# Values of three narrow attentions projected token-major and read back from DRAM into their block-diagonal tile

## What is computed

```python
qkv = x @ qkv_w.T + qkv_b                                  # [64, 17, 576]
qkv = qkv.reshape(B, N, 3, NUM_HEADS, hd).transpose(2, 0, 3, 1, 4)
q, k, v = (qkv[0], qkv[1], qkv[2])                         # 12 heads, hd = 16
attn = jax.nn.softmax(jnp.einsum('bhnd,bhmd->bhnm', q, k) * scale, axis=-1)
out = jnp.einsum('bhnm,bhmd->bhnd', attn, v)
out = out.transpose(0, 2, 1, 3).reshape(B, N, C) @ proj_w.T + proj_b
```

## Time and profile before

| | |
|---|---|
| median of 3 runs | 937.37 us (935.59 to 946.7) |
| the profiled execution | 934.18 us |
| its span | 932.1 us |
| stage a0 in the span | about 39 to 147 us |
| stage a2 | about 554 to 637 us |
| stage a3 | about 727 to 839 us |
| PE busy, DVE busy, ACT busy | 92%, 48%, 42% |

### The profile page before, as it was taken

The page is one execution under the profiler, slowest core; times in us unless marked ns, Lnnn a source line. Parts: engine busy times, 40 slices in busy tenths (PEclk is TensorE's granted clock), DMA queues, the critical chain, the costliest instruction groups (busy, mean ns, idle before and its releaser), DMA issues. The chain is left out here.

```text
span 932.1 us, 16890 instructions
## 1 busy us (share of the span) xinstructions
PE 854.9 (92%) x6194; PEld 608.5 (65%) x6195; DVE 447.4 (48%) x903; ACT 387.8 (42%) x857; POOL 186.7 (20%) x207
## 2 busy tenths in 40 slices
PE   6899888999998799999989789999999999999997
PEld 5556656677775467777668466765687566666776
DVE  5566676777744412222268666551104566633111
ACT  2366653453542022333243864554151455532332
POOL 0610003444500134445200012220000000002232
PEclk9999999999988899999999999999999999997999
DMA  8000000000004967112150019000000211102111
GB/s 294 1 2 1 1 2 0 1 2 1 1 2 102 256 182 198 46 51 46 39 164 3 0 45 258 6 2 28 1 1 1 56 50 50 52 19 97 43 51 34
DMA packets 30638, 51.07 MB, mean 55 GB/s; under 512 B 3750, under 2 KB 23752, under 8 KB 30572
## 3 DMA queue, kind: packets, MB, share of 16 engines
q1 hardware_dynamic: 22140, 36.09, 14.0%
q0 software_dynamic: 4416, 9.84, 3.8%
q10 hardware_dynamic: 4016, 4.23, 1.4%
HBM read 43.30 MB, written 6.83 MB: 54 GB/s over the span
## 5 line engine op out<-in xcount | busy, mean ns | idle before, releaser
L79 PE MATMUL banks<-con 128*128 128x512 f32 (+1 forms) x206 | 95.1, 572 | 3.0 <-DVEq L2136 1.4
L1846 PE MATMUL banks<-moe_wu,moe_xf 96*128 x256 | 92.1, 505 | 1.6 <-ACT moe_xf L1954 0.8
L634 PE MATMUL banks<-x,a_wqkv 96*96 96x272 f32 x288 | 74.6, 397 | 0.9 <-PEq L457 0.5
L1846 PEld LDWEIGHTS banks<-moe_wu,moe_xf 96*128 96x128 f32 x256 | 47.5, 195 | 31.4 <-issue 4.8
L944 ACT ACTIVATE a_vt<-banks 102x384 f32<-102x384 f32 x96 | 41.9, 488 | 50.4 <-PE banks L710 50.1
L154 ACT ACTIVATE ln_sq<-x 96x544 f32<-96x544 f32 x32 | 21.1, 658 | 93.2 <-DVE x L146 93.2
L634 PEld LDWEIGHTS banks<-x,a_wqkv 96*96 96x96 f32 x288 | 45.4, 164 | 18.2 <-issue 3.2
L79 PEld LDWEIGHTS banks<-con 128*128 128x128 f32 x206 | 38.4, 202 | 25.9 <-issue 22.4
L2151 DVE TENSOR_TENSOR moe_hid<-banks,moe_gs 128x384 f32<-128x384 f32 x32 | 17.9, 558 | 77.6 <-PE banks L1846 77.6
L710 PE MATMUL banks<-con,a_vx 96*102 96x96 f32 x384 | 42.7, 253 | 7.4 <-ACT a_vt L944 6.1
L2008 POOL DMA_INDIRECT moe_xs<-moe_x_rows,moe_taken x32 | 31.2, 974 | 76.1 <-PE banks L1830 54.2
(11 more groups left out here) (409 smaller groups left out, 1772.2 us busy)
## 6 DMA issues: line engine op xcount, KB each, us to landing
moe_wu<-in_moe_up SPq DMA_DIRECT2D x16, 576.0 KB, 8.9
f_w<-in_f_e SPq DMA_DIRECT2D x10, 576.0 KB, 14.6
moe_wd<-in_moe_down SPq DMA_DIRECT2D x16, 288.0 KB, 9.9
patch_px<-in_patches SPq DMA_DIRECT2D x4, 768.0 KB, 9.4
f_wu<-in_f_up SPq DMA_DIRECT2D x4, 582.0 KB
f_wd<-in_f_down SPq DMA_DIRECT2D x4, 576.0 KB
f_x_rows<-f_xtok ACTq DMA_DIRECT2D x4, 384.0 KB, 3.4
a_wqkv<-in_a_wqkv SPq DMA_DIRECT2D x3, 432.0 KB, 8.3
```

What stands on the lines that cost most here:

```text
L79: self.nc.tensor.matmul(self.ps[bank][:, 0:width], self.ident, self.con[:, 0:width], start=True, stop=True)
L634: last = nc.tensor.matmul(ps[2 + m][0:HD, 0:CW], wqkv[:, a, j * D + m * HD:j * D + (m + 1) * HD], chunk(x, c)[:, a], start=a == 0, stop=a ...
L1846: last = nc.tensor.matmul(ps[2 + 2 * p + u][:, 0:BW], xf[0:KU[a], p, a], wu[0:KU[a], bass.ds(e, 1), a, u * BW:(u + 1) * BW].rearrange("p e ...
```

## The change

- `vx`, `spread_values`, `project_v`, `turn_values` and the copies of `take_values` are gone. In their place `values(n)` projects values token-major for 9 tiles of 128 tokens in five groups (2, 1, 2, 2, 2 tiles), x as the weights and `wqkv`'s 192 value columns as the moving tile, into one PSUM bank; ACT copies a group to `vtok` [128 tokens, 192] in one instruction.
- SP writes each tile to a DRAM tensor `v_rows` [1088, 192] (96 KB a tile, 48 KB the last) and then reads the values back into `vt`, which now holds two whole chunks, [102, 2, 16, 2, 96]. For each chunk and each of the 12 heads there are two DMAs: one of 16 tokens x 16 images and one of the 17th token x 16 images, in pieces of 64 bytes. A chunk's read-back is 24 DMAs with 3,264 pieces. The first chunk's are shared: 12 from SP, 12 from ACT.
- The parts of `vt` off the diagonal are zeroed once a stage, by two POOL memsets of 102 x 3072.
- Columns of keys, scores and weights are ordered token by head (k h) and not head by token, so that the rows of `vt` of one head are 6 partitions apart. Maxima and sums of DVE read with a stride of 6; in a3 the sum is split in two.
- The loads of `ahead` are split into four parts, one issued at the head of each chunk on SP, between the read-back of that chunk and the writes for the next.
- In a3 the transposes of x have a step and a bank of their own (`turn_inputs`, `take_inputs`).

The diff, cut to its core:

```diff
+VTILES = [128 * t for t in range(T // 128)] + [T - 128]
+VGROUPS = [(0, 1), (2,), (3, 4), (5, 6), (7, 8)]
+VTILES_OF = [3, 5, 7, 9]
 class ClassWeights(Weights):
+    PARTS = ((0, 1), (2, 3), (4,), (5,))
...
-        for i in range(6):
+    def load_part(self, sp, part):
+        if part == 0:
+            sp.dma_start(self.gw[:], self.dram["gw"]).then_inc(self.gw_in, 16)
+        for i in self.PARTS[part]:
...
 class RouterWeights(Weights):
+    def load_part(self, sp, part):
+        if part == 0:
+            self.load(sp)
...
 class ExpertWeights(Weights):
+    def load_part(self, sp, part):
+        self.load(sp, range(part, part + 1))
...
+        def read_values(eng, c, parts):
+            if c < 2:
+                eng.wait_ge(vt_zero, c + 1)
+            else:
+                eng.wait_ge(ctx_ready, GPC * (c - 1))
+            src = v_rows[c * CW:(c + 1) * CW, :].rearrange("(i k) (a h d) -> k i a h d", k=N, a=2, h=HH)
+            for a in parts:
+                for h in range(HH):
+                    eng.dma_start(vt[h:(N - 1) * HH:HH, c % 2, :, a, h * HW:(h + 1) * HW], src[0:N - 1, :, a, h]).then_inc(v_in[c % 2], 16)
+                    eng.dma_start(vt[(N - 1) * HH + h:(N - 1) * HH + h + 1, c % 2, :, a, h * HW:(h + 1) * HW], src[N - 1:N, :, a, h]).then_inc(v_in[c % 2], 16)
+
         @block.sync
         def _(sp):
-            for w in ahead:
-                w.load(sp)
+            def write_values(n):
+                sp.wait_ge(v_taken, n + 1)
+                t, w = VGROUPS[n][0], len(VGROUPS[n])
+                for u in range(t, t + w - (t + w == len(VTILES))):
+                    sp.dma_start(v_rows[u * 128:(u + 1) * 128, :], vtok[:, u]).then_inc(v_written, 16)
+                if t + w == len(VTILES):
+                    sp.dma_start(v_rows[LAST_V:T, :], vtok[LAST_V - VTILES[-1]:128, t + w - 1]).then_inc(v_written, 16)
+
+            for n in range(2):
+                write_values(n)
+            sp.wait_ge(v_written, 16 * 3)
+            read_values(sp, 0, (0,))
+            for c in range(NC):
+                for w in ahead:
+                    w.load_part(sp, c)
+                if c + 1 < NC:
+                    write_values(c + 2)
+                    sp.wait_ge(v_written, 16 * min(VTILES_OF[c + 1], len(VTILES)))
+                    read_values(sp, c + 1, range(2))
...
+            def values(n):
+                if n >= 1:
+                    pe.wait_ge(v_taken, n)
...
+                for j, t in enumerate(VGROUPS[n]):
+                    for a in range(2):
+                        last = nc.tensor.matmul(v_bank[:, j * D:(j + 1) * D], x[:, a, VTILES[t]:VTILES[t] + 128], wqkv[:, a, 2 * D:3 * D],
+                                                start=a == 0, stop=a == 1)
+                last.then_inc(v_proj, 1)
...
             def weigh(g):
+                c = g // GPC
                 pe.wait_ge(pt_evicted, g + 1)
-                pe.wait_ge(vt_evicted, (g + 1) * FV)
+                if g % GPC == 0:
+                    pe.wait_ge(v_in[c % 2], 16 * 4 * HH * (c // 2 + 1))
...
+            values(0)
+            if quantum:
                 states()
             project_k(0)
+            values(1)
...
-            for m in range(2):
-                project_v(0, m)
...
-                turn_values(2 * c)
+                if quantum:
+                    if c == 0:
+                        pe.wait_ge(s_factor, 1)
+                    turn_inputs(2 * c)
+                if more:
+                    values(c + 2)
...
-                turn_values(2 * c + 1)
+                if quantum:
+                    turn_inputs(2 * c + 1)
...
-                if more:
-                    project_v(c + 1, 0)
...
-                    project_v(c + 1, 1)
...
+            def take_values(n):
+                act.wait_ge(v_proj, n + 1)
+                t, w = VGROUPS[n][0], len(VGROUPS[n])
+                nc.scalar.activation(vtok[:, t:t + w].rearrange("p t d -> p (t d)"), v_bank[:, 0:w * D], ACT.Copy).then_inc(v_taken, 1)
...
+            act.wait_ge(v_written, 16 * VTILES_OF[0])
+            read_values(act, 0, (1,))
             for c in range(NC):
                 more = c + 1 < NC
                 if quantum:
                     square_overlaps(2 * c)
-                take_values(2 * c)
+                    take_inputs(2 * c)
+                if more:
+                    take_values(c + 2)
                 exponent(2 * c)
...
+            for c in range(2):
+                pool.memset(vt[:, c], 0.0).then_inc(vt_zero, 1)
+                if c == 0 and response is not None:
+                    response.on_pool(pool, 1)
...
-            spread_values(0)
...
-                    spread_values(c + 1)
                     shift(2 * c + 2)
```

More of the change, by code:

```diff
@@ L570, in stage_narrow_attention @@
         k = sb("k", [HD, 2, 2, CW])
[L571 to L577, removed]
+        kx = sb("kx", [HD, 2, 2, IC, N * HH])
+        vtok = sb("vtok", [128, len(VTILES), D])
+        vt = sb("vt", [N * HH, 2, IC, 2, HD])
+        PC = 4 * HH * N
+        p = sb("p", [128, 2, 2 * HP * N])
+        pt = sb("pt", [N * HH, 2, 4, 128])
+        mx = sb("mx", [128, 2, 2 * HP])
+        sm = sb("sm", [128, 2, 2 * HP])
+        v_rows = nc.dram_tensor(name + "_v_rows", (T, D), F32).ap()
         ct = sb("ct", [128, 2, 2, D])
@@ L647, in project_q @@
                     project(c, 0, q_proj, m)
-            def project_v(c, m):
-                pe.wait_ge(qk_evicted, NT * c + 2 + m + 1)
-                project(c, 2, v_proj, m)
+            def values(n):
+                if n >= 1:
+                    pe.wait_ge(v_taken, n)
+                if VGROUPS[n][-1] >= 6:
+                    for c in carried:
+                        pe.wait_ge(before.ready, c + 1)
+                for j, t in enumerate(VGROUPS[n]):
[3 more added lines that the diff above has]
+                last.then_inc(v_proj, 1)
             def states():
@@ L695, in scores, with turn_inputs @@
                 last.then_inc(scored, 1)
[L697 to L705, removed]
-                        pe.wait_ge(vt_evicted, n - 1)
-                    for i in range(2):
-                        for a in range(2):
-                            o = (2 * i + a) * HD
-                            last = nc.tensor.transpose(ps[5 + n % 2][0:HH * N, o:o + HD],
-                                                       vx[:, c % 2, a, (g % GPC) * GI + 2 * f + i, :], env.ident[0:HD, 0:HD])
-                    last.then_inc(vt_ready, 1)
-                if quantum:
-                    n = g * FV + FV - 1
-                    pe.wait_ge(vt_evicted, n - 1)
-                    for f in range(2):
-                        for a in range(2):
-                            o = (g * GI + 4 * f) * N
-                            last = nc.tensor.transpose(ps[5 + n % 2][0:4 * N, (2 * f + a) * HD:(2 * f + a + 1) * HD],
-                                                       x[:, a, o:o + 4 * N], env.ident[0:HD, 0:HD])
-                    last.then_inc(vt_ready, 1)
+            def turn_inputs(g):
+                if g == 0:
+                    pe.wait_ge(s_taken, 1)
+                else:
+                    pe.wait_ge(xt_taken, g)
+                for f in range(2):
+                    for a in range(2):
+                        o = (g * GI + 4 * f) * N
+                        last = nc.tensor.transpose(ps[6][0:4 * N, (2 * f + a) * HD:(2 * f + a + 1) * HD],
+                                                   x[:, a, o:o + 4 * N], env.ident[0:HD, 0:HD])
+                last.then_inc(xt_ready, 1)
             def turn_weights(g):
@@ L747, in weigh @@
                                                 pt[:, g % 2, 2 * (i // 4) + a, SLOT * (i % 4):SLOT * (i % 4 + 1)],
[L748 removed]
+                                                vt[:, c % 2, (g % GPC) * GI + i, a, :], start=True, stop=True)
                 last.then_inc(ctx_ready, 1)
```

99 lines of the change are left out of this document (45 added, 54 removed).

## The result

The changed kernel takes 1029.96 us (median, 1025.68 to 1035.32) against 940.48 of the kernel before in the same series (935.59 to 946.7): ratio 1.095, 95% interval 1.086 to 1.104. It is slower by about 90 us, where 42 were forecast. The profiled execution takes 1025.68 us against 934.18, 91.5 more. (Some executions of a kernel are slower than its fastest by over 1.5%, at a lower clock: ratios leave them out, medians hold them, and the profiles of `no_dram`, `loads_last` and `loads_end` fell in such executions.)

A forecast was written before the change was run, and what follows sets the result against it. PE was taken to bound the kernel. Terms of -8.9 us (a0), +7 and +2 (a2), +40.1 and +2 (a3) gave +42.2 on 934.2, or 976.4; the forecast was 977, range 945 to 1018.

The forecast's parts named there:

- So a0's gain stands: In a0, values are projected some 30 us before use and take about 18 us, so 8.9 us are gained.
- The issue of a read: On SP, each read-back DMA takes 0.47 us to issue, so a chunk's 24 reads take 11.3 us.
- PE's work leaves: On PE, 5.6 us a chunk removed and 1.4 added: net 4.2 us a chunk, 3.7 in the last.
- second rival: Reads cost more than their issues (piece 80 ns or more, or issue 0.8 us): 1,020 us in all; chance 14%.
- a2's cycle: In a2, loads, write and reads on SP put the third chunk's values 24.1 us on; a2 loses about 7.
- The first chunk's issues on ACT: In a0's first chunk, 12 read issues hold ACT about 5.9 us, in time in which it idles now.
- a3's cycle: In a3, `wu` on one DMA engine holds the writes: 38.3 us a chunk against 24.1, fourth chunk 40.1 late.
- The clock behind the last wait: Idle PE drops to the lower clock; 2 us added behind the last wait of a2 and a3 each.
- Write 2.3 us: A 96 KB tile written to `v_rows` takes 2.3 us to land, and SP waits for it.
- DVE's stride: DVE's maxima and sums with changed stride cost nothing; bounds nothing and twice the 0.6 us of each.
- The first (the values are not held): Writes and reads pass the loads, so values are on time in every stage: 24 us faster, 910 us; chance 12%.
- The third (held half as much, +20 in a3): Loads hold values in a3 only partly: a3 +20 us instead of +40, 955 us in all; chance 8%.

The follow-up runs named there:

- no_dram: Changed kernel without writing the values to `v_rows` or reading them back, so `vt` stays zero; 953.4 us, 1.009 times the kernel before.
- loads_last: Changed kernel with `wu` loaded in two pieces and each chunk's next-stage loads issued behind its reads, not ahead of its writes; 979.9 us.
- loads_end: Changed kernel with `wu` loaded in two pieces and all next-stage loads issued behind the stage's last read; 980.9 and 963.6 us in two executions.
- nodram_fill: Changed kernel without writing or reading back the values, plus idle PE products in a0, a2 and a3; 917.6 us, 0.978 times the kernel before.
- best: Changed kernel with `wu` in two pieces, 12 reads a chunk, idle PE products and loads behind each chunk's reads; 917.5 us, 0.979 times the kernel before.
- merged: Changed kernel with `wu` in two pieces and one read serving both feature halves, 12 reads a chunk instead of 24; 955.9 us.

## Why the prediction was wrong

The direction was right, and so was the mechanism in a3 and a2. The sum was +42.2 us and the profiled difference is +91.5; of the 49 us between them a0 has 15, a2 15 and a3 20. Two steps failed. "So a0's gain stands" is wrong in kind: behind PE's grown waits the clock fell. The issue of a read, 0.47 us in the sum, is wrong in size: it takes 0.64 to 0.66, and an estimate from SP's rows puts most of the 35 us of a2 and a3 on it (in a3 4.1 to 4.6 us in each of three chunks and 3.1 in the first, 16 of 20). Either alone would have left the time within the stated range. The steps in turn:

- **PE's work leaves: right, but only at full clock.** The step says net 4.2 us a chunk and, after the waits, 8.9 in a0 and about 7 and 8 in the others. `nodram_fill` shows 4.6, 5.9 and 10.5; in a0 it has the 10 us at 0.50 in it. Eight matmuls of 192 columns took 1.5 us, 1.4 were taken.
- **a0: the mechanism failed.** "So a0's gain stands" looked at the values alone, and rightly: a chunk's last read is issued 9.3 us or more ahead of its `weigh`. What it missed is that `project_v` stood inside waits of PE. With a half of it (1.08 us) gone from each, the waits grew from 0.97 and 1.60 to 2.19 and 2.83 us, and behind them the clock fell. a0 came out at +6.3 instead of -8.9; with the gaps filled it is -4.2. The part on the clock did take an idle PE and a fall to 0.50 from the earlier trace rows, but asked only of the long waits for values and not of the short ones that the change makes longer.
- **The issue: mis-sized.** 0.47 us was read from the loads of `w1` and `w2`. The reads take 0.64 to 0.66 each, so 24 take 15.4 to 15.9 us and not 11.3. "SP busy over 0.6 us per read" was the prediction's own sign for its second rival. Put into a2's cycle, 9.0 + 2.2 + 15.8 + 1.6 - 0.8 = 27.8 us for the third chunk and 4.5 less for the fourth, 23.3: measured are 27.7 and 23.4 between the first reads. The structure of that sum was right and this term explains it.
- **The first chunk's issues on ACT: costed at nothing in a2 and a3.** The text put 5.9 us of ACT's issues into idle time, for a0, where it nearly holds (`weigh` 1.0 us later). In a2 `weigh` of the first chunk is 22.9 us after the start (17.5 before), in a3 28.9 (23.1); without the reads, in `no_dram`, it is 16.4 and 22.7. ACT's timeline in a3 has the last issue and what stood behind it:

```profile
775.63 0.63 ACTq L647 DMA_DIRECT2D a_vt<-a_v_rows  x1
776.31 0.23 ACT L975 ACTIVATE a_osq<-banks 128x68 f32<-128x68 f32 x1 [8.22 <-issue]
```

- **a3's cycle: right but for the same term.** Taken 38.3 us, with 15.9 for the reads 42.9; measured between `wu` issues are 45.2, 43.2 and 43.3. The second chunk was to come 11 us late and came 20.7 late (67.3 against 46.6 from the start): the first pair is issued 20.7 us after the start instead of 16.3, since the 12 reads ahead of it take 8.7 us and not 5.6 and start 1.4 us later, and the 24 reads behind it take 4.6 us more. Fourth: 59.5 late instead of 40.1.
- **The clock behind the last wait: right.** From the fourth `weigh` to the stage's end 17.4 us became 20.0 in a3 and 9.7 became 11.4 in a2; 2 each were taken.
- **Write 2.3 us: right on an empty queue** (1.7 landed, plus its issue), 5 to 10 from its last issue to the first read behind loads, which the sum carried as the load's own 9.0 or 4.5 us.
- **DVE's stride: within its bounds.** The sums over 408 columns from SBUF went from 567 to 879 ns (24 times), the maxima from PSUM from 575 to 580. DVE held by POOL's memset, 4 us in a3, stood in no term.

Of the rivals, the second (an issue of 0.8 us, 1,020 us) names the term that was wrong, with the other half of its reason (a slow piece) false. The first (the values are not held) forecasts 24 us less than before: `nodram_fill` and `best` have 20 and 22 less, but only with the gaps filled; `no_dram`, where nothing is held, gains nothing. The third (held half as much, +20 in a3) is refuted by a3's +62. What stood in no rival is the clock in a0, and the first chunk's issues on ACT.

## What to carry to other kernels

Before work is taken from the engine that sets the pace, look at which of its waits the work was standing in: the wait grows by what is taken out, and behind the grown waits (2.2 to 2.8 us here) the granted clock was 0.50 for 7 to 24 us, which cost more than the work had. Count small DMAs by their issues on the queue that carries them, with the price of their own form, and keep them out of the queue behind weights, above all behind a tensor whose partition count puts it on one DMA engine. A change that is slower as a whole can hold a gain: here it needed `wu` cut in two, half the issues and a few idle products.

## What the runs showed of the hardware

- Pieces of 64 bytes are cheap. In the window 590 to 594 us of the changed kernel only reads move: 14 GB/s at a share of 0.16 are 219 pieces per us for 2.56 busy engines, 12 ns a piece; in `merged` 29 GB/s at 0.31, 11 ns. The row of 96-byte pieces had given 24. The Trainium skill (*DMA: Bandwidth & Descriptors*, specifications) puts the least transfer for full rate at 512 bytes, and the trace agrees: 64 bytes in 12 ns are 5 GB/s an engine, against 20 for the 768-byte pieces of the earlier trace rows. It costs nothing here, since 204 pieces on an engine take 2.4 us and their issues 15.4.

```profile
590.00:594.00 4.00, 4.00 (x42) 3.28 (x34) 2.07 (x4) 0.45 (x3) 0.00 (x0) 1.00 0.16 14
```

- A read of 16 partitions and one of 1 partition, 256 and 16 pieces, cost the same to issue (0.60 and 0.61 us, 0.64 apart), and so do those of 512 and 32 pieces in `merged` (12 in 7.79 us, 0.65 each).
- What a short wait of PE can cost: behind each of the three waits of 2.16 us of a3 in `no_dram` stands a stretch at 0.50 of 20 to 24 us, in which PE is busy for 97% at half its speed. The kernel before had one low window in a0, 0.62 from 120 to 124 us, behind a wait of 1.60 us; the same wait a chunk earlier had none behind it.

```profile
795.00:819.00 24.00, 23.31 (x162) 17.53 (x163) 7.94 (x22) 6.87 (x15) 0.00 (x0) 0.50 0.14 48
```

- Two `TENSOR_SCALAR` instructions of DVE, 0.15 and 0.23 us by themselves, took 3.9 and 4.0 us while POOL ran its memset.
